# Kernel row of a Toeplitz convolution: taken as a 129th column of another product, turned once, stored from a new place in SyncE's queue

## The reference

```python
x = x + einsum('bct,bcd->bdt', x, weights[condition])            # layer 0
# layer 1, on the new x; K is the convolution kernel of each channel h
dtA = (-exp(log_A_real) + 1j * A_imag) * exp(log_dt)[:, None]
Cs  = Cc * (exp(dtA) - 1.0) / A
K   = 2.0 * einsum('hn,hnl->hl', Cs, exp(dtA[:, :, None] * arange(L))).real
u_m = u * mask
y   = irfft(rfft(u_m, 2L) * rfft(K, 2L))[..., :L] + u_m * D[:, None]
x = x + y * mask
```

## Time and profile before

| | us |
|---|---|
| median of 3 runs | 2274.95 |
| the three runs | 2273.8, 2274.95, 2285.9 |
| profiled execution, its own time | 2279.22 |
| its span | 2277.6 |

### The profile page before, as it was taken

One profiled execution on the slowest core, in us unless ns is written; L12 is line 12 of the kernel. 1 busy time (PEld: TensorE's weight loads), 2 busy tenths in 40 slices (PEclk: granted clock), 3 DMA queues, 4 the chain that ended last, 5 costly groups with the idle time before them and its releaser, 6 DMA issues.

```text
span 2277.6 us, 62956 instructions
## 1 busy us (share of the span) xinstructions
PE 2141.6 (94%) x15101; PEld 1885.9 (83%) x15101; DVE 1596.3 (70%) x3359; ACT 1437.4 (63%) x4107; POOL 1314.7 (58%) x2115
## 2 busy tenths in 40 slices
PE   5877778999999999999999999899999999999999
PEld 2222226988889999998989889799999999999999
DVE  4999303777777777777777768577777777777776
ACT  4556556777767777777777777455555555555555
POOL 0995504877778878887888777333333333333330
PEclk9999998999999999999999999999999999999999
DMA  8999999999999999999999999888888888999887
GB/s 313 420 419 387 407 375 334 336 326 326 323 320 341 336 334 340 337 340 330 336 327 337 323 326 327 246 253 269 272 273 263 277 269 260 271 272 268 275 264 230
DMA packets 347685, 716.28 MB, mean 314 GB/s; under 512 B 41602, under 2 KB 172932, under 8 KB 347652
## 3 DMA queue, kind: packets, MB, share of 16 engines
q1 hardware_dynamic: 282116, 480.99, 67.8%
q10 hardware_dynamic: 55296, 201.35, 22.5%
q0 software_dynamic: 10240, 33.56, 3.8%
HBM read 395.92 MB, written 319.82 MB: 314 GB/s over the span
## 4 chain that ended last, share of the span: by engine, by line
PE 49%; DMA 28%; SPq 8%; issue 5%; ACT 4%; ACTq 3%; DVE 2%; DVEq 0%
DMA out<-decay 17%; PE bank L926 10%; PE bank L927 10%; PE bank L928 10%; PE bank L971 6%; SPq L341 5%; PE bank L963 5%; PE bank L908 4%; DMA row_x<-in_x 4%; DMA decay<-x_scratch 4%; PE bank L895 3%; ACTq L545 2%; DMA toep<-k_scratch 2%; DVE decay L829 2%; DMA x_scratch<-row_y 1%
## 5 line engine op out<-in xcount | busy, mean ns | idle before, releaser
L817 DVE TENSOR_TENSOR u_lo<-bank,u_hi 128x512 fp32r<-128x512 f32 x512 | 354.2, 692 | 201.7 <-ACT u_hi L621 198.7
L562 ACT ACTIVATE row_y<-bank 128x512 f32<-128x512 f32 x512 | 301.7, 589 | 216.1 <-PE bank L928 115.2
L829 DVE COPY_PREDICATED decay<-mask,bank 128x512 f32<-128x512 uint8 x512 | 379.2, 741 | 44.6 <-PE bank L928 36.4
L971 PE MATMUL bank<-toep,u_odd 128*128 128x128 f32 x2048 | 393.5, 274 | 0.0
L926 PE MATMUL bank<-t_hi,u_hi 128*128 128x256 f32 x1024 | 354.9, 347 | 16.3 <-DMA toep<-k_scratch 16.3
L509 POOL TENSOR_TENSOR x_lo<-row_x,x_hi 128x256 fp32r<-128x256 f32 x496 | 361.7, 760 | 0.0
L478 POOL COPY par<-table 128x71 f32 (+1 forms) x256 | 72.1, 282 | 491.0 <-DVE e_lo L812 489.8
L481 POOL TENSOR_TENSOR outer<-par 128x256 f32<-128x256 f32 x512 | 335.8, 676 | 21.1
L895 PE MATMUL bank<-row_x,w_sel 128*128 128x512 f32 x528 | 263.2, 625 | 87.2 <-DMA row_x<-in_x 52.0
L823 DVE TENSOR_TENSOR s_lo<-state,s_hi 128x128 fp32r<-128x128 f32 x768 | 295.1, 384 | 52.2 <-ACT s_hi L633 51.1
L971 PEld LDWEIGHTS bank<-toep,u_odd 128*128 128x128 f32 x2048 | 313.8, 189 | 0.0
(11 more groups left out here) (141 smaller groups left out, 5314.5 us busy)
## 6 DMA issues: line engine op xcount, KB each, us to landing
row_x<-in_x SPq DMA_DIRECT2D x256, 512.0 KB, 7.5
x_scratch<-row_y ACTq DMA_DIRECT2D x256, 512.0 KB, 7.1
decay<-x_scratch SPq DMA_DIRECT2D x256, 512.0 KB, 6.0
out<-decay SPq DMA_DIRECT2D x256, 256.0 KB, 5.5
out<-decay ACTq DMA_DIRECT2D x128, 512.0 KB, 5.6
t_hi<-k_scratch SPq DMA_DIRECT2D x256, 128.0 KB, 4.8
t_lo<-k_scratch SPq DMA_DIRECT2D x256, 128.0 KB, 4.5
b_scratch<-b_mat POOLq DMA_DIRECT2D x128, 256.0 KB, 5.7
```

Of the source, the lines that this page charges most:

```text
L817: v.tensor_tensor(u_lo[j % 2][:, blocks, :], t_bank[q][:, :].rearrange("s (k b) -> s k b", b=B), u_hi[j % 2][:, blocks, :].bitcast(fp32), ...
L829: v.copy_predicated(tile[j][:, cols], mask[:, seg * SEG + q * BANK:seg * SEG + (q + 1) * BANK], y_bank[q][:, :]).then_inc(y_taken, 1)
L971: mm(y[:, P:CHUNK], u_odd[i][:, c, :], toep[j][:, P - 1::-1], start=False, stop=True, skip_group_check=True)
```

## The change

- make_mats no longer makes k_part with three matmuls. m_mat gets a 129th column, the channel's column of ck_all (copied there by POOL), so that L921's product gives b_part and, in a 129th column of each of its two parts, K's values 128 to a part, one per partition. PE no longer waits for e_split there, but for k_ready of the channel before.
- keep_k becomes one DVE operation of 128 x 32 that writes 16 copies of these two columns, with D + 1 added, into k_cols; a third column per copy stays zero. It waits for ACT's b_half; ACT's keep_b no longer waits for DVE.
- turn_k is a new fp32r transpose of 128 x 128 on PE, behind chunk 0 of the following channel. Its result, 48 x 128 in the same bank, is k_rows.
- split_k (two copies and a subtraction of 48 x 128) takes the place of halve_k and split_k on DVE, behind split_s(1) of the following channel.
- k_scratch holds the same values in three planes of 16 x 384; the store has 48 x 3 pieces of 512 bytes. The loads of the Toeplitz matrix read the same pieces as before.
- SP issues store_kernel(k + 2) behind load_toeplitz(k + 1) and ahead of the second half of channel k - 1, where store_kernel(k + 3) stood at the channel's end, ahead of load_x1.
- In the rows alone, PE now makes one transpose ahead of its second make_mats, and SP stores only one kernel row at the place where it stored two.

```diff
@@ SP
-            for k in range(2):
-                store_kernel(k, k)
+            store_kernel(0, 0)
...
-            store_kernel(2, 2)
+            store_kernel(1, 1)
...
                     if then[0] == 1:
                         load_toeplitz(1, k + 2, j2, then[2])
+                    if then[0] == 0:
+                        store_kernel(k + 2, j2)
                     if not (isinstance(k, int) and k == 0):
                         store_x2_half(k - 1, j3, 1)
...
-                    if third[0] == 0:
-                        store_kernel(k + 3, j3)
@@ store_kernel
-                sp.dma_start(k_dram[bass.ds(k, 1), :, :].rearrange("a s w -> (a s) w"), k_rows[i][:, :, :].rearrange("s n w -> s (n w)")).then_inc(k_stored[i], 16)
+                sp.dma_start(k_dram[bass.ds(k, 1), :, :, :].rearrange("a n s w -> (a s) n w"), k_rows[i][:, :, :]).then_inc(k_stored[i], 16)
@@ DVE
             def keep_k(k, j):
-                i = j % 2
-                dve.wait_ge(gen_made, k + 1)
+                dve.wait_ge(b_half, k + 1)
+                if isinstance(k, int) and k == 0:
+                    dve.wait_ge(pad_zeroed, 1)
+                else:
+                    dve.wait_ge(k_turned, k)
+                columns = k_cols[:, 0:KCOPIES].rearrange("p (s n) -> p s n", n=KROW // P)
+                v.tensor_tensor(columns[:, :, 0:2], k_part.unsqueeze(1).to_broadcast([P, COPIES, 2]),
+                                par[j][:, COL_DP:COL_DP + 2].unsqueeze(1).to_broadcast([P, COPIES, 2]), ALU.add).then_inc(k_kept, 1)
+
+            def split_k(k, j):
+                i, row = j % 2, k_rows[j % 2]
+                dve.wait_ge(k_turned, k + 1)
                 if not (isinstance(k, int) and k < 2):
                     dve.wait_ge(k_stored[i], k * 8 - i * 8)
+                v.tensor_copy(row[:, 1, :].bitcast(fp32r), k_turn).then_inc(k_half, 1)
+                v.tensor_copy(row[:, 0, :], k_turn)
                 dve.wait_ge(k_half, k + 1)
+                v.tensor_tensor(row[:, 2, :].bitcast(fp32r), k_turn, row[:, 1, :], ALU.subtract).then_inc(k_ready, 1)
@@ PE, make_mats
-                pe.wait_ge(e_split, k + 1)
                 if not (isinstance(k, int) and k == 0):
                     pe.wait_ge(b_ready, k)
-                split_mm(k_part, ck[j][:, 0:1].to_broadcast([P, P]), ck[j][:, 1:2].to_broadcast([P, P]), e_hi[j][:, :], e_lo[j][:, :], start=True, stop=True)
+                    pe.wait_ge(k_ready, k)
                 for p in range(2):
-                    ins = mm(b_part[:, p, :], e_mat[j][:, p * P:(p + 1) * P], m_mat[i][:, :], start=True, stop=True)
+                    ins = mm(gen_part[:, p, :], e_mat[j][:, p * P:(p + 1) * P], m_mat[i][:, :], start=True, stop=True)
                 ins.then_inc(gen_made, 1)
+
+            def turn_k(k, j):
+                pe.wait_ge(k_kept, k + 1)
+                pe.wait_ge(b_ready, k + 1)
+                nc.tensor.transpose(gen_bank[:, BANK - P:BANK].bitcast(fp32r), k_cols_r[:, :], eye_r[:, :]).then_inc(k_turned, 1)
```

More of the change, by code:

```diff
@@ L120, in s4d_program @@
         halves = sb("halves", [P, N])
-        m_mat = [sb(f"m_mat{i}", [P, P]) for i in range(2)]
+        m_mat = [sb(f"m_mat{i}", [P, P + 1]) for i in range(2)]
         r_mat = [sb(f"r_mat{i}", [P, P]) for i in range(SLOTS)]
-        ck_all = sb("ck_all", [P, H, 2], fp32r)
-        ck = [sb(f"ck{i}", [P, 2], fp32r) for i in range(SLOTS)]
+        ck_all = sb("ck_all", [P, H])
         b_mat = [sb(f"b_mat{i}", [P, 2, 2, P], fp32r) for i in range(SLOTS)]
         b_hi, b_lo = [b[:, 0, :, :] for b in b_mat], [b[:, 1, :, :] for b in b_mat]
-        k_rows = [sb(f"k_rows{i}", [COPIES, 3, KROW]) for i in range(2)]
+        k_rows = [sb(f"k_rows{i}", [KCOPIES, 3, P]) for i in range(2)]
         toep = [sb(f"toep{i}", [P, P]) for i in range(SLOTS)]
@@ L464, in _ @@
             link(pool.tensor_scalar(table[:, :, COL_R + 1], table[:, :, COL_P2 + HIGH - 1], -1.0, None, ALU.mult))
-            link(pool.tensor_scalar(table[:, :, COL_DP], d_bc[:, :], 1.0, None, ALU.add))
-            pool.wait_ge(ck_split, 1)
+            link(pool.tensor_scalar(d_bc[:, :], d_bc[:, :], 1.0, None, ALU.add))
+            link(pool.memset(table[:, :, COL_DP], 0.0))
+            link(pool.tensor_tensor(table[:, :, COL_DP + 1], d_bc[:, :], eye[:, P - 1:P].to_broadcast([P, H]), ALU.mult))
+            pool.memset(k_cols, 0.0).then_inc(pad_zeroed, 1)
             def make_e(seg, k, j):
                 if not (isinstance(k, int) and k < SLOTS):
-                    pool.wait_ge(gen_made, k - 3 if seg == 0 else H)
-                    pool.wait_ge(k_made, k - 3 if seg == 0 else H)
+                    pool.wait_ge(gen_made, k - 1 if seg == 0 else H)
+                    pool.wait_ge(k_kept, k - 3 if seg == 0 else H)
                     pool.wait_ge(e_split, k - 3)
@@ L490, in _ @@
                     pool.wait_ge(e_ready, e_before(0, k))
+                if k >= 2:
+                    pool.wait_ge(gen_made, k - 1)
                 make_e(0, k, k)
@@ L584, in keep_parameters @@
                 last.then_inc(turned_kept, 1)
-                nc.scalar.activation(ck_all[:, :, 0], bank[5][:, 0:P], ACT.Copy).then_inc(turned_kept, 1)
+                nc.scalar.activation(ck_all[:, :], bank[5][:, 0:P], ACT.Copy).then_inc(turned_kept, 1)
             def make_sines(half):
@@ L842, in _ @@
                     split_e(2, 2)
+                if k < 2:
+                    split_k(k, k)
             for q in range(NQ):
@@ L850, in channels @@
                     after, third = later(g, j, seg, 1), later(g, j, seg, 3)
+                    then = later(g, j, seg, 2)
                     makes = third and third[0] == 0
@@ L858, in channels @@
                     split_s(seg, k, j, 1)
+                    if then and then[0] == 0:
+                        split_k(k + 2, (j + 2) % SLOTS)
                     if after:
@@ L863, in channels @@
                         split_u(k + 1, j1, 1)
-                    if makes:
-                        keep_k(k + 3, j3)
                     split_s(seg, k, j, 3)
@@ L868, in channels @@
                     if makes:
-                        halve_k(k + 3, j3)
+                        keep_k(k + 3, j3)
                         split_b(k + 3, j3)
-                        split_k(k + 3, j3)
                     if third and seg == 1:
@@ L981, in channels @@
                     k = g * SLOTS + j
-                    j1, j3 = (j + 1) % SLOTS, (j + 3) % SLOTS
-                    after, third = later(g, j, seg, 1), later(g, j, seg, 3)
+                    j1, j2, j3 = ((j + d) % SLOTS for d in (1, 2, 3))
+                    after, then, third = (later(g, j, seg, d) for d in (1, 2, 3))
                     drive(seg, k, j)
@@ L998, in channels @@
                             from_state(seg, k, j, c - 1)
+                        if c == 0 and then and then[0] == 0:
+                            turn_k(k + 2, j2)
                         if c == 0 and after:
@@ L1005, in channels, with second_matrices @@
                     from_state(seg, k, j, NCH - 1)
-            row_groups(pe, rows, None, turn_parameters, None, None, lambda: make_mats(0, 0), lambda: make_mats(1, 1))
+            def second_matrices():
+                pe.wait_ge(eye_made, 1)
+                pe.wait_ge(pad_zeroed, 1)
+                turn_k(0, 0)
+                make_mats(1, 1)
+            row_groups(pe, rows, None, turn_parameters, None, None, lambda: make_mats(0, 0), second_matrices)
+            turn_k(1, 1)
             make_mats(2, 2)
```

47 lines of the change are left out of this document (17 added, 30 removed).

## The result

The changed kernel takes 2325.34 us (median of 4 runs, 2313.54 to 2328.95) against 2276.61 us before: a ratio of 1.0217, with a 95% interval from 1.0183 to 1.025. It is slower, by 49 us where 27 were forecast.

The account below looks back on a forecast made before the run. Two loops of nearly equal length bound segment 0, SP's pacing 72% of channels. 2279 + 24 (kernel row in SP's loop) + 3 (start) = 2306 us, or 2302 on the median of 2275; range 2260 to 2345.

Parts of the forecast that it names:

- SP's loop: Segment 0: load_x1, Toeplitz loads, second half, then its landing, which frees the tile; 2.89 us issuing plus 5.50 landing.
- 72% of the channels: Segment 0: share said to be paced by SP's loop, from 84 load_x1 waits for a landing in 116 channels.
- 0.22 us a channel: Price of the kernel row inside SP's loop, segment 0; over 124 channels 27 us, counted as 24.
- the 72 KB ahead of the half: Kernel row's bytes in SP's queue, taken as what the half cannot escape: 0.22 us at 330 GB/s.
- the 0.63 us of issue: Kernel row's issue between load_x1 and the half; if landing stays 5.5 us, 78 us over 124 channels.
- the wait for k_ready: SP, ahead of the kernel row: no wait, 0.2 us to spare; rival case, 12 to 37 us, no separate chance.
- The rule on completion counts: The row's 144 small writes would hold the half's count: at least the 0.22, leaning to the slow end.
- PE's saving: PE's loop 0.35 us a channel shorter; rival that it shows: 2263 us, up to 43 us gained (2232), chance 0.18.
- the bounds of 0.6 to 1.2 us: DVE's four new operations per channel, between half the old ones' cost and all; 0.8 taken, not setting the pace.
- the 321.3 that I had worked out: Rows alone, second make_mats: time in us when PE gets there after waiting for k_ready of channel 0.
- The 3 us of the sum: Rows alone: cost added for PE's new stall at the second make_mats, between 0 and 5 us.
- The signs that I named: Segment 0 profile after: issuing 3.5 us, landing median 5.0 to 5.3, period near 8.75, PE about 92%; segment 1 unchanged.

Follow-up runs that it names:

- e6: Kernel before, with the second half of channel k - 1 issued directly behind load_x1, ahead of the Toeplitz loads: 2280.36 us, ratio 1.0013.
- e11: Changed kernel, with the half of channel k - 1 issued directly behind load_x1, ahead of the Toeplitz loads; kernel row still behind these: 2231.85 us, ratio 0.983.
- e2: Kernel before, with only the kernel row's store moved behind the Toeplitz loads and ahead of the half: 2329.2 us, ratio 1.024.
- e3: As e1, with a 512-byte DMA to a spare tensor added ahead of the half: 2335.38 us, ratio 1.0252.
- e9: Kernel before, with a 512-byte DMA to a spare tensor added behind the Toeplitz loads, ahead of the half: 2313.11 us, ratio 1.0204.
- e1: Changed kernel, with the kernel row issued behind the second half of channel k - 1 instead of ahead of it: 2306.54 us, ratio 1.0126.
- e4: As e1, with the three Toeplitz loads of channel k + 1 issued ahead of load_x1(k + 2): 2441.54 us, ratio 1.0742.
- e7: Changed kernel, with the kernel row's store moved from SP's queue to ACT's, behind ACT's second copy of u: 2295.1 us, ratio 1.0072.
- e8: As e7, with the half issued directly behind load_x1, ahead of the Toeplitz loads: 2260.51 us, ratio 0.9921.
- e10: Kernel before, with a 512-byte DMA added at the channel's end, ahead of store_kernel(k + 3) and load_x1: 2293.92 us, ratio 1.0106.
- e5: Kernel before, with the kernel row of k + 2 issued behind the second half of channel k - 1: 2296.36 us, ratio 1.0065.

## Why the prediction was right

**What bounds.** Two loops of nearly equal length. The 72% of the channels that I gave to SP's loop are a count of waits, short ones too; in the chain of the kernel before, matmuls have 46% from 450 to 1440 us and the landing of out<-decay with SP's issues most of the rest, so the two share the time about evenly. e6 and e11 confirm both: with SP's loop out of the way the chain is matmuls, and on the old work nothing is gained, since PE's loop is as long.

**The mechanism.** The kernel row goes from a place that is mostly covered to one inside SP's loop. e2 shows it: the place alone gives the loss.

**The size was off.** I forecast 0.22 us a channel and it was 0.43 by the period (8.53 to 8.96). The term that failed is the one that took the price from the 72 KB ahead of the half and let the queue absorb the 0.63 us of issue. Measured, the half comes 0.77 us later after load_x1, and the rest of the loop is 0.34 us shorter. The share that is absorbed is 44% of it, not two thirds, and 0.27 us of the 0.34 are a shorter landing of the half (5.29 to 5.02). The bytes, which I made the whole price, are not what makes it: e3 and e9 show that an issue of 512 bytes does most of the same. Of the 0.77 us, 0.70 are the issue: from the kernel row to the half it is 0.72 in the mean and 0.63, as forecast, in the median. The other 7.4 / 111 = 0.07 are the wait for k_ready, which I had put at none; DVE's three operations took 0.82 us (276 + 271 + 271 ns) and not 0.65, which uses up most of the 0.2 us that I saw to spare. The forecast counted 124 channels at 0.22 and took off a little; 0.43 times 124 is 53 us, close to the 51 found in segment 0. So the time lies in the range by the right loop and by the width of the range; the price in the sum was half of the measured one, and the argument that gave it does not hold.

**The rule on completion counts.** By the Trainium skill's rule on completion counts (DMA: Bandwidth & Descriptors, "Queues, rings and completion order") the small writes ahead would hold the half, and the sum would lean to the slow end. It did lean there, but the runs give no support to that reason: counted from its issue, the half landed after 5.02 us with the 144 writes of the row ahead of it and after 5.00 with 16 writes (e2, e9), and after 5.29 with none between the Toeplitz loads and it (before).

**PE's saving.** 0.35 us a channel was the estimate from the distances of matmuls, 0.30 is what e6 and e11 show. It was hidden, as forecast, because PE was not the longer loop.

**DVE.** Its four operations take 276 + 271 + 271 + 175 = 993 ns, inside the bounds of 0.6 to 1.2 us, above the 0.8 that I took. In the changed kernel by form (busy us, mean ns, idle before):

```profile
L804 DVE CAST k_rows<-bank 48x128 fp32r<-48x128 f32 x110 | 30.4, 276 | 36.2 <-PE bank L929 36.1
L805 DVE COPY k_rows<-bank 48x128 f32<-48x128 f32 x110 | 29.8, 271 | 0.0
L807 DVE TENSOR_TENSOR k_rows<-bank,k_rows 48x128 fp32r<-48x128 f32 x110 | 29.8, 271 | 0.0
L796 DVE TENSOR_TENSOR decay<-bank,par 128x32 f32<-128x32 f32 x111 | 19.4, 175 | 0.0
```

**The start.** The stall is where it was foreseen, at the second make_mats, in time:

```profile
317.37 0.43 DVE L815 TENSOR_TENSOR e_lo<-e_mat,e_hi 128x256 fp32r<-128x256 f32 x1 [7.02 <-ACT e_hi L605]
317.71 0.28 DVE L804 CAST k_rows<-bank 48x128 fp32r<-48x128 f32 x1
...
318.52 1.20 PE L922 MATMUL bank<-m_mat,e_mat 128*128 128x129 f32 x4 [4.84 <-DVE k_rows L807]
```

PE waited 4.84 us for split_k(0), queued behind split_e(2). That is 2.8 us earlier than the 321.3 that I had worked out, since ACT's e_hi came earlier here. What it cost does not show: the first load_x1 of segment 0 came at 358.76 instead of 357.44, but with the same program ahead of it this start lies between 354.5 and 360.4 in e1, e3, e4, e7, e8 and e11, and between 357.4 and 367.0 in before, e6, e9 and e10. The 3 us of the sum are neither confirmed nor refuted.

**The signs that I named.** Issuing at 3.5 us: 3.72. Period near 8.75: 8.96. PE's share 92%: 93%. Segment 1 kept its time. Median landing of 5.0 to 5.3: the view of issues has 5.8 for both halves together, and I had not separated the two. Taken apart by their place in SP's order, the second half, which frees the tile, lands after 5.05 us in the median, and it was 5.22 before; the first half of a channel, which now stands closer behind the row load, lands after 6.56 instead of 5.65. So this sign came in for the half that matters, but the kernel before had it too. The chain: matmuls fell from 46% of it to 16% (450 to 1440 us), but stretches without SP's loop were left, the longest of 38 us from 546.7 us.

**What stays open.** Why the row behind the half costs 0.65% on the old work (e5), with issuing as before and no wait for its landing. And why 512 bytes ahead of load_x1 cost 1% (e10). In both it is the half itself that lands 0.2 to 0.3 us later after its issue. No run separates a longer queue from a different meeting with the other queues' DMAs.

## What to carry to other kernels

Where a buffer is freed by a DMA's landing and refilled from the same queue, everything issued between the refill and the next such DMA is part of a loop whose length is issuing plus landing. Put nothing there that can stand elsewhere, not even 512 bytes (2.0% in e9), and issue the DMA that frees the buffer first. Before moving a store, look also at who waits for its landing: the row's short lead on its loads spoiled e4. And when work taken off one engine brings nothing, look for the loop that hides it before giving the work up: the same change was 2.2% slower or 1.7% faster by the place of one store.

## What I had not expected of the hardware

- A DMA of 512 bytes added to SP's loop costs nearly as much as one of 72 KB moved into it (e9 1.0204, e2 1.024), and an added one also costs something in a place where SP mostly waits (e10, 1.0106).
- DVE's making of m_mat (128 x 128) went from 309 ns to 706 in the mean, although it does the same. In the changed kernel POOL's make_e starts beside it, and the operation ahead of it, the same in form, takes 0.27 us in some channels and 0.70 in others, with POOL's product beside it in both:

```profile
1007.60 1.39 POOL L482 TENSOR_TENSOR outer<-par 128x256 f32<-128x256 f32 x2
1007.61 0.27 DVE L782 TENSOR_TENSOR r_mat<-halves,par 128x128 f32<-128x128 f32 x1
1007.80 0.71 DVE L782 TENSOR_TENSOR m_mat<-halves,par 128x128 f32<-128x128 f32 x1
...
1015.69 1.25 POOL L482 TENSOR_TENSOR outer<-par 128x256 f32<-128x256 f32 x2
1015.76 0.70 DVE L782 TENSOR_TENSOR r_mat<-halves,par 128x128 f32<-128x128 f32 x1
1016.38 0.71 DVE L782 TENSOR_TENSOR m_mat<-halves,par 128x128 f32<-128x128 f32 x1
```

An operation that begins 0.01 us behind POOL's took 0.27 us, one that begins 0.07 us behind it 0.70. It is the same for r_mat throughout the trace from 440 to 1440 us: all 82 operations that began within 0.02 us of POOL's product were short, all 27 that began later, during it, were long. DVE had room for it (72% busy), and no run tries it alone, so that POOL is the cause is an argument from these times and not shown.
